# A graph layer and a mixture of experts in one kernel: zero products ahead of the first stage's work, a new order of its first products, a later root, and 16-bit tables

## The reference

```
def gnn(x, W1, b1, W2, b2, src, dst):          # x is layer-normalised first
    feat = concat([x[dst], x[src] - x[dst]])   # 512 wide
    h = relu(feat @ W1 + b1)                   # 512 wide
    msg = h @ W2 + b2                          # 256 wide
    return segment_sum(msg, dst) / (degree + 1e-8)

def ffn(x, gamma, beta, Wr, br, W1, b1, W2, b2):   # x is layer-normalised first
    xn = layernorm(x) * gamma + beta
    w = softmax of the two largest of xn @ Wr + br, 8 experts
    return sum over the two chosen e of w[e] * (gelu(xn @ W1[e] + b1[e]) @ W2[e] + b2[e])

x = x + gnn(layernorm(x), ...)
x = x + ffn(layernorm(x), ...)
```

## Time and profile before

| | |
|---|---|
| Time, median of 3 runs | 1121.46 us |
| The three runs | 1121.46, 1126.88, 1121.32 us |
| Span of the profiled execution | 902.9 us |
| Median time less that span | 218.6 us |
| Mean granted TensorE clock over the span | 0.995 |
| Busy: PE, DVE, ACT, POOL | 834.7, 651.0, 628.3, 602.4 us |
| Block A, to the last product | 0 to 65.1 us |
| First and last start of the gathers in block B | 66.3 and 581.1 us |

### The profile page before, as it was taken

How to read it: one execution, slowest core, us unless ns; L and a number is a source line. 1 busy time by engine, 2 the same in 40 slices (tenths; PEclk the granted TensorE clock), 3 DMA queues, 4 the chain that set the end, 5 groups by cost and what they waited for, 6 DMA issues and landing times. The chain is left out here.

```text
span 902.9 us, 17755 instructions
## 1 busy us (share of the span) xinstructions
PE 834.7 (92%) x4088; PEld 652.2 (72%) x4089; DVE 651.0 (72%) x1764; ACT 628.3 (70%) x1393; POOL 602.4 (67%) x615
## 2 busy tenths in 40 slices
PE   6997999999999989989999999989999999999997
PEld 3444767767676666766666666768888999999996
DVE  6846888888888888878888887756894455455443
ACT  4425788888888888888898889845554555555553
POOL 2317777777777777777777777659404677776764
PEclk9998999999999999999999999999999999999999
DMA  8547777878888778888887878819852344444443
GB/s 255 171 150 220 247 239 245 247 234 251 240 243 236 247 231 243 241 238 238 245 248 235 230 233 264 228 49 281 265 139 54 59 73 75 81 71 68 76 71 45
DMA packets 91000, 169.47 MB, mean 188 GB/s; under 512 B 17604, under 2 KB 56910, under 8 KB 90840
## 3 DMA queue, kind: packets, MB, share of 16 engines
q0 software_dynamic: 43696, 122.35, 49.8%
q1 hardware_dynamic: 46232, 44.79, 17.0%
q10 hardware_dynamic: 944, 0.92, 0.4%
HBM read 146.98 MB, written 21.43 MB: 187 GB/s over the span
## 5 line engine op out<-in xcount | busy, mean ns | idle before, releaser
L1001 POOL DMA_INDIRECT gath<-q_rows,idx_t x408 | 391.9, 960 | 138.8 <-issue 93.3
L1068 DVE SCALAR_TENSOR_TENSOR h_lo<-bank,h_hi 128x512 fp32r<-128x512 f32 x327 | 219.4, 682 | 40.1 <-ACT h_hi L1250 38.0
L1250 ACT ACTIVATE h_hi<-bank 128x512 fp32r<-128x512 f32 x327 | 191.0, 598 | 45.5 <-DVE bank L1063 20.9
L1231 ACT ACTIVATE bank<-gath 128x512 f32<-128x512 f32 x287 | 173.4, 604 | 14.3 <-DMA gath<-q_rows,idx_t 10.5
L1384 PE MATMUL bank<-p_hi,ohT 128*128 x287 | 123.4, 430 | 42.8 <-ACT bank L1231 40.3
L1428 PE MATMUL agg_ps<-h_hi,oh 128*128 128x512 f32 x408 | 161.9, 397 | 0.3 <-DVE h_lo L1068 0.2
L1429 PE MATMUL agg_ps<-h_lo,oh 128*128 128x512 f32 x408 | 161.3, 395 | 0.0
L1995 POOL DMA_INDIRECT out<-y_out,sca_i x56 | 93.7, 1673 | 49.0 <-issue 15.9
L1384 PEld LDWEIGHTS bank<-p_hi,ohT 128*128 128x128 f32 x287 | 54.1, 189 | 91.2 <-issue 83.0
L1385 PE MATMUL bank<-p_lo,ohT 128*128 x287 | 113.9, 397 | 0.0
L2099 PE MATMUL bank<-tokT,fw_now 128*128 128x128 f32 x896 | 109.3, 275 | 0.8 <-ACT tokT L2055 0.8
(11 more groups left out here) (287 smaller groups left out, 1276.6 us busy)
## 6 DMA issues: line engine op xcount, KB each, us to landing
rows_sb<-rel_blocks SPq DMA_DIRECT2D x102, 128.0 KB, 4.3
fw<-in_L_ffn_W SPq DMA_DIRECT2D x16, 512.0 KB, 5.1
gath<-q_rows,idx_t POOLq DMA_INDIRECT x408, 4.4
q_rows<-q_buf SPq DMA_DIRECT2D x25, 256.0 KB, 2.4
out<-x_all SPq DMA_DIRECT2D x28, 128.0 KB, 3.8
x_all<-in_x SPq DMA_DIRECT2D x25, 128.0 KB, 2.7
xm_rows<-xt SPq DMA_DIRECT2D x25, 128.0 KB, 3.0
x_all<-in_x SPq DMA_DIRECT2D x2, 640.0 KB, 10.3
```

Source lines behind the costliest of these rows:

```text
L1001: pool.indirect_dma_start(out=gath[:, j % RING, :], out_offset=None, in_=q_rows[:, :], in_offset=bass.IndirectOffsetOnAxis(ap=idx_t[:, j:j ...
L1068: dve.scalar_tensor_tensor(out=h_lo[:, j % LO_RING, :], in0=z_of(slot0, j), scalar=0.0, in1=h_hi[:, j % HI_RING, :].bitcast(F32), op0=ALU. ...
L1231: actv.activation(z_of(slot0, j), gath[:, j % RING, :], ACT.Copy).then_inc(s_seed, 1)
L1250: actv.activation(h_hi[:, j % HI_RING, :], z_of(slot0, j), ACT.Relu).then_inc(s_hi, 1)
```

## The change

Five edits:

- POOL writes `zero_r` first and not among its last constants. TensorE waits for it and makes 18 products of zeros (`FIRST_WAKE`) ahead of its first turn, and 3 more (`NEXT_WAKE`) between the first turn and the first product. They go to the second bank of `deg_ps`.
- TensorE takes turns 1 and 2 and then product 1 at once. The count (L782) and turn 3, which stood ahead of product 1, stand ahead of product 2. Turns 4 and 5 both stand ahead of product 3, and from product 4 on the order is the old one.
- ACT copies turns 1 and 2 ahead of root 2 (before: root 2, then turn 1, and turn 2 behind the normalising of tile 3). DVE inverts part 2 ahead of `count_firsts`.
- The roots of the parts have steps of their own. Only part 6 moves, from step 12 to step 14.
- `tile_of_slot`, `tile_row`, `tile4_i`, `group_tile` and `turn_i` are of 16-bit and no longer of 32-bit integers.

```
-    tile_of_slot = nc.dram_tensor("tile_of_slot", (SC, P), I32, kind="Internal").ap()
+    tile_of_slot = nc.dram_tensor("tile_of_slot", (SC, P), U16, kind="Internal").ap()
...
-        tile_row = sb("tile_row", [1, SC * P], I32, edge_ctx)
+        tile_row = sb("tile_row", [1, SC * P], U16, edge_ctx)
...
-        tile4_i = sb("tile4_i", [SC, P], I32, b_ctx)
+        tile4_i = sb("tile4_i", [SC, P], U16, b_ctx)
...
-        group_tile = sb("group_tile", [NG, GROUP], I32, b_ctx)
+        group_tile = sb("group_tile", [NG, GROUP], U16, b_ctx)
...
-        turn_i = sb("turn_i", [P, 2, MS], I32)
+        turn_i = sb("turn_i", [P, 2, MS], U16)
...
+        ROOTS_AT = {3: 2, 4: 4, 5: 7, 6: 14, 7: 16}
...
             def _(pool):
+                pool.memset(zero_r[:].bitcast(F32), 0.0).then_inc(s_bc, 1)
                 pool.memset(ones_mat[:], 1.0).then_inc(s_const, 1)
...
-                pool.memset(zero_r[:].bitcast(F32), 0.0).then_inc(s_bc, 1)
...
                 statistics(2)
+                invert(2)
                 count_firsts()
-                invert(2)
...
-                        if t == STATS_AT[k] + 1:
+                        if t == ROOTS_AT[k]:
                             invert(k)
...
                 normalise(2)
+                turn(1)
+                turn(2)
                 root(2)
-                turn(1)
                 normalise(3)
                 for t in range(NT):
-                    if t + 2 < NT:
+                    if 2 < t + 2 < NT:
                         turn(t + 2)
                     for k in range(3, len(parts)):
-                        if t == STATS_AT[k] + 1:
+                        if t == ROOTS_AT[k]:
                             root(k)
...
-                pe.wait_ge(s_const, 4)
+                def zero_products(n):
+                    for _ in range(n):
+                        pe.matmul(deg_ps[:, 1, :], zero_r[:], zero_r[:].unsqueeze(1).to_broadcast([P, KH, P]), start=True, stop=True)
+
...
+                pe.wait_ge(s_bc, 1)
+                zero_products(FIRST_WAKE)
+                pe.wait_ge(s_const, 4)
                 turn(0)
+                zero_products(NEXT_WAKE)
                 pe.wait_ge(s_w[1], 16)
                 for t in range(NT):
                     if t == 1:
                         turn(1)
                         turn(2)
+                    if t == 2:
                         pe.wait_ge(s_cnt, 1)
                         pe.matmul(deg_ps[0:NT, 1, 0:1], first_lt[0:ER, 0:NT], ones_mat[0:ER, 0:1], start=True, stop=True).then_inc(s_cnt_sum, 1)
-                    if t and t + 2 < NT:
+                    if t in (2, 3):
+                        turn(t + 1)
+                    if t > 2 and t + 2 < NT:
                         turn(t + 2)
                     product_q(t)
```

More of the change, by code:

```diff
@@ L23 @@
 BF16 = mybir.dt.bfloat16
+U16 = mybir.dt.uint16
 ALU = mybir.AluOpType
@@ L37 @@
 WAKE, CONST_AT = 2, 4
+FIRST_WAKE, NEXT_WAKE = 18, 3
 READY, PARTS = 2, 2
```

## The result

| | before | after |
|---|---|---|
| Time, median | 1122.38 us (4 runs, 1121.32 to 1126.88) | 1112.73 us (4 runs, 1107.56 to 1117.02) |
| Ratio, 95% interval | | 0.9888 [0.9845, 0.993] |
| Profiled execution: its own time, span | -, 902.9 us | 1117.02, 1115.2 us |
| Mean granted TensorE clock | 0.995 | 0.907 |
| First and last gather | 66.3 and 581.1 us | 63.9 and 773.2 us |

What follows compares the result with a forecast made beforehand. POOL's gathers were taken to set block B's length and TensorE's chain in block A its beginning. 2.35 + 0.57 - 0.3 = 2.6 us off 1121.46 gave 1118.9 us, range 1116.5 to 1123.0.

Steps and rivals of the forecast that it cites:

- What bounds the kernel: POOL's gathers, 1.265 us apart, set block B's length; TensorE's chain in block A sets its beginning.
- around the span: 218.6 us put outside the profile's 902.9 us span; the profiled execution's own time was taken as 1121.46 us.
- step 5: 16-bit tables: register loads cost the same, hidden by the gathers' pace; smaller transfers at most 0.4 us; taken as 0.
- Step 1: Block A's beginning: zero products from about 1.2 us raise the clock, so product 0 runs at full clock, 8.65 to 10.4.
- Step 2: Block A's new order: product 2 starts at 13.35 instead of 15.69; 2.35 us gained, bounds 1.6 to 2.9.
- Step 3: Block A, before turn 16: moving root 6 two steps later removes TensorE's idle 0.57 us; 0.57 us gained.
- Step 4: Block A: DVE comes only 0.8 us earlier, TensorE 2.35; two slacks just hold; 0.3 us taken off for latencies.
- sums of counts: Block A: ready at 23.54, TensorE gets there at 25.16; 1.6 us of slack, of which 1.55 is used.
- The first table: Behind product 21: ready at 52.68, TensorE there at 55.19; slack 2.5 us less 0.2, of which 2.1 is used.
- one off the whole: A microsecond off TensorE's chain in block A should take one microsecond off the whole kernel.
- the threshold: Block B: TensorE's spare 0.37 us in four slots; beyond it each 0.1 us per load costs 10 us.
- dearer loads: Rival: 16-bit loads, at 1.5 us each, exceed what TensorE has to spare in block B; 13 us, 1135; chance 0.04.

Runs made afterwards that it cites:

- k2: The changed kernel with all five tables back at 32 bits and waits using max(tile, 0), against before on a 904 us chip: 902.3 us, ratio 0.9978.
- e2: The changed kernel with the five tables at 32 bits and waits using max(tile, 0), against before at 1107.32 us: ratio 0.997.
- j1: The changed kernel as it is, against before on a 904 us chip: 957.3 us, ratio 1.0574.
- a1: Before with the zero products alone, 32-bit tables and waits using max(tile, 0), on a 904 us chip: first gather at 67.57 us.
- a2: The changed kernel without zero products, with 32-bit tables and waits using max(tile, 0), on a 904 us chip: first gather at 65.14 us.
- j2: Before with waits using max(tile, 0) and only ACT's loads in 16 bits, on a 904 us chip: ratio 1.064, span 953.3 us.
- j3: Before with waits using max(tile, 0) and nothing else, on a 904 us chip: ratio 1.0003, span 902.5 us.
- l1: Before with waits using max(tile, 0), ACT making each 32-bit load of seventeen tiles twice, both read, against before at 1127.78 us: ratio 0.9981.
- e4: Before with waits using max(tile, 0) and nothing else, against before at 1107.32 us: ratio 0.9989, span 1106.6 us.

## Why the prediction was wrong

**What bounds the kernel.** Right for a 904 us chip, and wrong for the chips that were timed. There POOL doesn't set block B's pace, nor is the clock full: the 218.6 us that I left "around the span" were the sign, and I explained them away by giving the profiled execution a time that its span contradicts. The busy shares and the distance of the gathers were those of another kind of chip than the one whose time I had to predict. And neither kind gave the ratio that I forecast (0.9977): the change has 0.9888 on the timed chip and 1.0574 on a 904 us chip, because of step 5. Steps 1 to 4 alone, `k2`, have 0.9978 on a 904 us chip.

**Step 1, the zero products.** Right. They started at 1.04 (predicted 1.2), turn 0 at 7.49 (7.7), product 0 at 8.43 (8.65), its four records within 1.96 us (1.9). The zero products start 0.43 us apart up to 5.5 us and 0.23 us apart from 5.9 us on, and the first stretch with a record of full clock begins at 5.8 us: inside my bounds (5.0 to 7.9) and a little before the middle that I took (6.4). It varies by more than I allowed: in e2 it rose at 4.1 us, before my early bound, in j1 at 6.9 us. What the step lacks is that the clock must be kept as well: a1 shows it fall again behind product 0, after two idle times of 1.06 and 0.70 us. On the page "TensorE: Matmul & The Clock Gate", section "What's actually happening", the Trainium skill has sustained work release the clock; the 18 products of zeros agree with it, which no row of before could show.

**Step 2, the order.** Right: product 1 at 11.08 (11.2), product 2 at 13.41 (13.35). But 0.22 us of the gain at product 2 is not one: turn 4 stood ahead of product 2 and now stands behind it. And I costed steps 1 and 2 as one sum; apart they are worth -1.3 (a1) and, with step 3, +1.1 us (a2).

**Step 3, root 6.** Right. TensorE goes from product 13, which starts at 35.56, to turn 16, the first row here, and on without idle time:

```profile
37.28 0.38 PE L761 MATMUL bank<-ident,xn_buf 128*128 128x128 f32 x2
37.50 1.88 PE L768 MATMUL bank<-w1g,x_all 128*128 128x512 f32 x4
39.22 0.38 PE L761 MATMUL bank<-ident,xn_buf 128*128 128x128 f32 x2
39.43 1.88 PE L768 MATMUL bank<-w1g,x_all 128*128 128x512 f32 x4
```

**Step 4, what comes due.** Right within its size. TensorE won 2.28 us up to product 2 and 0.79 at turn 16 (products 13 and 14 start 1.94 us apart instead of 2.73). Of these 3.07 us 2.41 arrived at the last pair. Turn 4 took the 0.22 us just named, 0.33 went at the sums of counts and 0.12 at product 9; I had taken 0.3 for all that comes due. The sums of counts, answering:

```profile
22.98 0.23 DVE L561 TENSOR_SCALAR cnt<-ident,start_col 25x25 f32<-25x25 f32 x1
```

```profile
23.32 0.41 PE L802 MATMUL deg_ps<-cnt,ones_mat 125*128 125x32 f32 x2
```

DVE ends at 23.21 and TensorE starts at 23.32: the 1.6 us of slack are used up. The first table took nothing (products 21 and 22 start 2.81 us apart, as before). In k2 and e2 3.1 us arrived at the first gather, in j1 1.9. At the end of the kernel it is less: k2's 0.9978 is 2.0 us [1.1, 2.9], so "one off the whole" for each microsecond was a little too much.

**Step 5, the 16-bit tables.** This step failed: its term was put at nothing, and it is by far the largest. "Nearest is the same load; the gathers' pace hides it" was twice wrong. ACT's load went from 1.26 to 3.59 us, and TensorE's, for which I had worked out the threshold, didn't change (0.99). ACT's queue I had not costed at all: 2.3 us for each of the five loads in 100 us is 11.6 us, nearly all of the 14.6 us of 100 that ACT is idle in the earlier trace rows, and that would have been a rival of its own. On a 904 us chip it costs 51 us (j2 against j3), so the "dearer loads" rival was the right kind of answer for the profile's chip, with the wrong engine. On the timed kind of chip the same load gives about 1% (0.9889 for the tables alone, 0.9899 for ACT's loads alone). In the result itself it is what block A leaves of the 9.65 us, about 7 us (an estimate, since the 2.41 us of block A are read against a trace from the other kind of chip), and that put the median below my range: without it 1122.38 - 2.4 = 1120.0 us would have lain inside. That the miss is a gain is the chip's doing; on the profile's own kind the same term is a loss of 5.7%.

**What stays open.** Why a longer stand of ACT's queue helps there. The trace of after shows what such a chip is like, around 132 us:

```profile
132.18 0.39 PE L1442 MATMUL agg_ps<-h_hi,oh 128*128 128x512 f32 x1
132.41 0.39 PE L1443 MATMUL agg_ps<-h_lo,oh 128*128 128x512 f32 x1
134.29 0.60 ACT L1264 ACTIVATE h_hi<-bank 128x512 fp32r<-128x512 f32 x1 [2.31 <-PE agg_ps L1443]
134.50 0.49 DVE L1070 TENSOR_SCALAR ohT<-rows_sb,slot_no 128x512 fp32r<-128x512 bf16 x1 [1.80 <-remote]
...
135.62 0.79 PE L1398 MATMUL bank<-p_hi,ohT 128*128 x1 [2.82 <-ACT bank L1245]
```

TensorE's product ends at 132.80, and ACT, which waits for it, moves at 134.29. In this trace that semaphore has three updates within 0.24 us, the first at 134.21; in j1, on a 904 us chip, each is 0.01 to 0.02 us behind the end of its product. TensorE then waits for ACT in turn, the clock falls, and the first products behind the gap are slow (0.79 instead of 0.39 us). A stand of ACT's queue might let several such late signals pass in one wait instead of in several; that is argued and not shown, and l1 didn't decide it. Something else of the 16-bit load isn't excluded there. Nor does any run show why one kind of chip passes TensorE's signals on late.

## What to carry to other kernels

Compare the span of a profile with the time to be predicted before anything else. Here 1.8 to 1.9 us lay around every span; if the difference is much larger, the profile is of another execution or chip, and no busy share in it may carry a forecast for the timed one. Cost a register load by its form on each engine's queue and not on the one that looks tight: here 17 narrow entries took 3.6 us where 17 wide ones took 1.25, and the gain of block A (0.2 to 0.3%) is had on both kinds of chip only with the wide ones. Products that raise the clock paid here only with an order behind them that leaves no idle time in which it falls.

## What was unexpected of the hardware

- The same kernel takes 904 us on two chips (three sets: 904.02, 903.61, 904.22) and 1107 to 1128 us on others (1107.32, 1108.11, 1122.38, 1127.78). Block A and the experts' stages hardly differ (first gather at 66.3 and 65.9 us, last edge sum to the end 309.0 us in both before and e4); the 408 gathers take 514 and 708 us.
- On the second kind of chip the traces hold only 303 to 325 updates of the semaphore that counts the edge sums, on the first kind all 410. The ends of matmuls are modelled, but ACT acts on TensorE's signal late as well (1.49 us in the rows above, 132.80 to 134.29).
- A register load's time depends on the number and the width of its entries: 4 tiles on TensorE 1.00 us (32 bits) and 0.99 (16 bits), 17 tiles on ACT 1.25 and 3.59, on either kind of chip (medians). The Trainium skill, on the page "Runtime: NRT & Kernel Launch", section "The launch sequence", gives about 1.3 us for a `TENSOR_LOAD`, but for one that loads registers from HBM ahead of the kernel. No run here shows that one; the loads here are the kernel's own, from SBUF.
- One and the same edit (ACT's loads in 16 bits) is 0.990 on one kind of chip and 1.062 to 1.064 on the other.
